# Flamingo block with routed experts: the last sums are taken into the experts' block

## What is computed

```python
x = x + tanh(g_xattn) * attention(layernorm(x), ctx)
t = layernorm(x)
top_w, top_i = top_k(softmax(t @ gate_w.T + gate_b), 2)
y = sum over the two choices of top_w * expert[top_i](t)
z = shared_expert(t)
x = x + tanh(g_ffn) * (y + z)
```

## Time and profile before

| | us |
|---|---|
| median of 3 runs | 618.12 |
| lowest, highest | 616.40, 619.42 |
| the profiled execution's own time | 621.78 |
| its span, first to last instruction | 619.8 |

### The profile page before, as it was taken

One profiled execution on the slowest core, in us unless ns is written; L12 is line 12 of the kernel. 1 busy time (PEld: TensorE's weight loads), 2 busy tenths in 40 slices (PEclk: granted clock), 3 DMA queues, 4 the chain that ended last, 5 costly groups with the idle time before them and its releaser, 6 DMA issues. The chain is left out here.

```text
span 619.8 us, 21883 instructions
## 1 busy us (share of the span) xinstructions
PE 491.7 (79%) x8747; PEld 415.3 (67%) x8747; DVE 417.3 (67%) x1246; ACT 324.5 (52%) x775; POOL 325.8 (53%) x454
## 2 busy tenths in 40 slices
PE   3889999899998998898776488999999999992000
PEld 2667777677777777776575377898889888982000
DVE  4677888688887888786933555676667666652166
ACT  2576877667776876775541224555555455552000
POOL 0012136466665675557777601776776776677000
PEclk9898999799999999998966599999999999997555
DMA  4222223334233243332112683466666665611398
GB/s 159 88 68 71 79 76 94 108 90 130 80 111 107 88 129 91 114 92 68 58 55 86 185 281 105 154 202 201 206 198 190 192 202 187 201 52 55 117 374 332
DMA packets 61221, 84.87 MB, mean 137 GB/s; under 512 B 11040, under 2 KB 36768, under 8 KB 60960
## 3 DMA queue, kind: packets, MB, share of 16 engines
q1 hardware_dynamic: 49552, 60.00, 31.3%
q0 software_dynamic: 8704, 17.97, 8.6%
q10 hardware_dynamic: 2864, 5.49, 2.5%
HBM read 52.89 MB, written 24.28 MB: 125 GB/s over the span
## 5 line engine op out<-in xcount | busy, mean ns | idle before, releaser
L1008 POOL DMA_INDIRECT expert_results<-YW,XB x144 | 138.1, 959 | 82.8 <-ACT YW L719 48.2
L957 POOL DMA_INDIRECT routed_rows<-STAGE,IDX x128 | 126.9, 991 | 41.6 <-issue 32.5
L719 ACT ACTIVATE YW<-YB,XB 128x128 f32<-128x128 f32 x144 | 46.0, 390 | 58.8 <-DVE YB L942 53.2
L628 ACT ACTIVATE PT<-BANKS 128x512 f32<-128x512 f32 x128 | 71.0, 614 | 8.6 <-PE BANKS L427 7.9
L427 PE MATMUL BANKS<-CST,LATE 128*128 128x128 f32 x512 | 73.9, 291 | 0.3 <-ACT PT L628 0.3
L427 PEld LDWEIGHTS BANKS<-CST,LATE 128*128 128x128 f32 x512 | 62.3, 150 | 10.9 <-issue 8.0
L970 POOL TENSOR_TENSOR VE<-MV,EPSV 128x4 f32<-128x4 f32 (+1 forms) x35 | 6.9, 196 | 116.9 <-DVE MV L755 116.8
L437 PE MATMUL BANKS<-VX,PT 128*32 128x18 f32 x4096 | 54.0, 188 | 10.5 <-issue 10.1
L760 DVE TENSOR_REDUCE MX<-BANKS 128x16 f32<-128x1024 f32 x32 | 39.1, 1222 | 30.0 <-PE BANKS L412 29.9
L628 ACT ACTIVATE VX<-BANKS 64x128 f32<-64x128 f32 x128 | 35.2, 275 | 45.6 <-PE BANKS L546 43.3
L437 PEld LDWEIGHTS BANKS<-VX,PT 128*32 128x32 f32 x4096 | 45.3, 112 | 19.4 <-issue 17.4
(11 more groups left out here) (113 smaller groups left out, 1032.8 us busy)
## 6 DMA issues: line engine op xcount, KB each, us to landing
LATE<-in_experts SPq DMA_DIRECT2D x72, 257.0 KB, 3.0
XB<-routed_rows SPq DMA_DIRECT2D x72, 130.0 KB, 3.0
XCT<-in_inputs_t SPq DMA_DIRECT2D x32, 256.0 KB, 2.9
YC<-expert_results SPq DMA_DIRECT2D x32, 256.0 KB, 5.8
X<-in_x SPq DMA_DIRECT2D x32, 128.0 KB, 3.1
LATE<-QK SPq DMA_DIRECT2D x128, 32.0 KB
out<-X ACTq DMA_DIRECT2D x16, 256.0 KB, 5.5
STAGE<-STAGE SPq DMA_DIRECT2D x6, 512.0 KB
```

The costliest lines, as they stand in the source:

```text
L628: return nc.scalar.activation(dst, src, ACT.Copy)
L719: nc.scalar.activation(YW[:, (j - 1) % 2, p, a, :], YB[:, p, a, :], ACT.Copy, scale=XB[:, (j - 1) % SLOTS, p, a, DIM:DIM + 1]).then_inc(yw ...
L957: nc.gpsimd.indirect_dma_start(routed[:, :], bass.IndirectOffsetOnAxis(ap=IDX[:, s, g.slots.start + t:g.slots.start + t + 1], axis=0), STA ...
L1008: nc.gpsimd.indirect_dma_start(results[:, :], bass.IndirectOffsetOnAxis(ap=XB[:, b, p, a, DIM + 1:DIM + 2].bitcast(i32), axis=0), YW[:, b ...
```

## The change

The second block is gone. Its three loops stand behind the experts' steps in the streams of SP, ACT and DVE of the first block, so that DRAIN and barrier between the two are gone as well.

- SP and ACT each wait for the eight sent semaphores (wait_results); POOL no longer does.
- YC and YSUM are views of the memory of STAGE, now one flat tensor STAGED of 6240 values on each partition, of which the views take 6144.
- The loads of the second choice (s = 1) of the first four steps are issued by ACT, and all others by SP as before.
- DVE's wait for out_ready of its own earlier step is dropped.
- The loops are written out over constants, with the same sixteen steps, sizes and four buffers.

```diff
-            STAGE = sa("STAGE", [128, TOPK, RING * UT, ROW])
+            STAGED = sa("STAGED", [128, TOPK * RING * UT * ROW])
+            STAGE = STAGED[:, :].rearrange("p (s r c) -> p s r c", s=TOPK, c=ROW)
+            wide = CBUFS * CG * DIM
+            YC = STAGED[:, 0:TOPK * wide].rearrange("p (b s a d) -> p b s a d", b=CBUFS, s=TOPK, d=DIM)
+            YSUM = STAGED[:, TOPK * wide:(TOPK + 1) * wide].rearrange("p (b a d) -> p b a d", b=CBUFS, d=DIM)
...
+            def load_results(engine, n, s):
+                engine.dma_start(YC[:, n % CBUFS, s, :, :], y_tiles[s, :, n * CG:(n + 1) * CG, :]).then_inc(y_in[n % CBUFS], 16)
+
+            def wait_results(engine):
+                for b in range(SLOTS):
+                    engine.wait_ge(sent[b], 64 * ((STEPS - b + SLOTS - 1) // SLOTS))
...
                 run_b(sp, expert_step)
+
+                wait_results(sp)
+                for n in range(CSTEPS):
+                    if n >= CBUFS:
+                        sp.wait_ge(ysum_done, n - CBUFS + 1)
+                    load_results(sp, n, 0)
+                    if n >= CBUFS:
+                        load_results(sp, n, 1)
...
                 run_b(act, expert_step)
 
+                wait_results(act)
+                for n in range(CBUFS):
+                    load_results(act, n, 1)
+                for n in range(CSTEPS):
+                    act.wait_ge(out_ready, n + 1)
+                    act.dma_start(out[:, n * CG:(n + 1) * CG, :], X[:, n * CG:(n + 1) * CG, :]).then_inc(stored, 16)
+                act.wait_ge(stored, 16 * CSTEPS)
...
                 run_b(dve, expert_step)
+
+                for n in range(CSTEPS):
+                    b = n % CBUFS
+                    dve.wait_ge(y_in[b], 32 * (n // CBUFS + 1))
+                    nc.vector.tensor_tensor(YSUM[:, b, :, :], YC[:, b, 0, :, :], YC[:, b, 1, :, :], ALU.add).then_inc(ysum_done, 1)
+                    here = X[:, n * CG:(n + 1) * CG, :]
+                    dve.wait_ge(ysum_done, n + 1)
+                    nc.vector.tensor_tensor(here, here, YSUM[:, b, :, :], ALU.add).then_inc(out_ready, 1)
...
                 run_b(pool, expert_step)
-                for b in range(SLOTS):
-                    pool.wait_ge(sent[b], 64 * ((STEPS - b + SLOTS - 1) // SLOTS))
```

More of the change, by code:

```diff
@@ L40 @@
 CG = 4
+CBUFS = 4
+CSTEPS = TILES // CG
 class Group:
@@ L246, in build_program @@
                  "yb_done", "yw_done", "sh_ready", "sgs_done", "hs_done", "z_ready", "zb_done", "x_done"))
+            y_in = [sem(f"y_in{b}") for b in range(CBUFS)]
+            ysum_done, out_ready, stored = sem("ysum_done"), sem("out_ready"), sem("stored")
+            y_tiles = results[0:TOPK * TOKENS, :].rearrange("(s p a) d -> s p a d", s=TOPK, p=128)
             block = own.enter_context(nc.Block())
+            def load_results(engine, n, s):
[3 more added lines that the diff above has]
+                    engine.wait_ge(sent[b], 64 * ((STEPS - b + SLOTS - 1) // SLOTS))
             def run(step):
```

## The result

The changed kernel takes 611.16 us (median of 8 runs, 607.25 to 613.63); the kernel before, with as many runs, takes 616.83 (614.69 to 620.42). The ratio is 0.9897, 95% interval 0.9863 to 0.9931: 4.3 to 8.5 us less. The profiled execution has a span of 609.0 us, against 619.8.

A forecast was written before the change was run, and what follows sets the result against it. It took an idle gap during POOL's DRAIN, slow first loads, then full DMA engines at 405 GB/s as the bounds. Gains 5.1 + 1.1 = 6.2 us, from median 618.12 to 611.9 us; range 608.5 to 615.5.

The forecast's parts named there:

- The hole: Between POOL's last scatter and the first load of YC: removing DRAIN and barrier gains 5.1 us, bounds 4.9 to 5.3.
- The hole stays: Before the first loads: the 4.65 us are not the DRAIN's own and remain; gain 1.6, 616.5 us, chance 0.09.
- DRAIN of some 4.6 us beside the loads: Sign expected in the profile after: POOL's DRAIN runs while the first loads move, not ahead of them.
- First loads on two queues: Start of the last sums: SP and ACT each issue four of eight first loads; gain 1.1 us, between 0 and 2.0.
- Taken: 290 GB/s: Rate assumed for the eight first loads: 2.95 MB at 10.3 us after first issue, 0.46 MB more, gain 1.1 us.
- both bounds: Limits for issuing the first loads from SP and ACT: gain 0 at 265 GB/s, 2.0 us at 395 GB/s.
- the upper bound: First loads at the kernel start's 395 GB/s: 3.30 MB at 10.3 us, 0.81 MB more, gain 2.0 us.
- barrier only: Last sums: reading limited at 265 GB/s, so faster issue only lengthens a queue; gain 5.1, 613.0 us, chance 0.24.
- Two queues are faster: First loads of the last sums: SP and ACT together reach the kernel start's 395 GB/s; gain 7.1, 611.0 us, chance 0.13.
- The slower case: Full DMA stretch: longer streams wait for their own instructions, three 7.9 us waits on SP; 623.6 us, chance 0.04.
- The waits on ACT: ACT waits for the sent semaphores before its four loads, its last product done ten us earlier; cost 0.
- the dropped wait of DVE: In the last sums, DVE's wait for its own sum of four steps earlier is removed; effect 0.

## Why the prediction was right, and where not

**The hole.** This part was right, in size and in cause. Foretold: 5.1 us, with 4.9 to 5.3 as bounds. Measured: 7.53 - 2.40 = 5.13 in the traces, and the same 7.53 or 7.54 in all four traces with two blocks, 2.40 to 2.42 in all traces where nothing waits for the DRAIN. That POOL's DRAIN is what fills it was an argument in the prediction and is shown now by putting it back: 4.8 of the 5.1 us return. "The hole stays" is out: the loads' data flow from 573.7 us on, 0.9 us after the first issue, while POOL's DRAIN lasts until 576.0. The sign "DRAIN of some 4.6 us beside the loads" came as one of 10.99 us, since it is recorded from before the last scatters.

**First loads on two queues.** This is the term that failed: 1.1 us foretold, and about 0.1 in the traces. From first load to end the three with one queue and no long issue take 36.3, 36.4 and 36.4 us, the four with four of the first loads on ACT and the same sums 36.0, 36.2, 36.4 and 36.5. By the medians 1.1 us is neither shown nor excluded. The step that went wrong is the one it was measured against: "Taken: 290 GB/s" and both bounds compare with 2.49 MB in the first ten us, and the 290 is itself the rate of that execution, the one with an issue of 1.79 us. Two others of the same kernel moved 3.03 and 3.04 MB, more than the 2.95 that two queues were to reach. What the prediction called in dispute, the rate with all eight loads issued, is 320 to 332 GB/s with one queue and 391 to 406 with two, near the 395 of the upper bound. A second queue does move more at first (3.17 to 3.25 MB against 2.91 to 3.04), 0.3 to 0.8 us at the full rate, but nothing of that can be seen at the last sum. Much of the lead is still there 32 us after the first issue, when 0.65 and 0.71 MB are left in the changed kernel and 0.78 and 0.82 in the later profiles of the kernel before; it goes in the last four us, where the DMA engines are no longer full (154 to 187 GB/s on the mean). The upper bound, 3.30 MB, wasn't reached in the changed kernel.

**The rivals.** What the runs show is most like "barrier only" in size, though not for its reason: 265 GB/s was no limit on reading, as one queue had 320 to 332 and two had 391 to 406. "Two queues are faster" holds for some ten us and not for the time. The rule of the Trainium skill, page "DMA: Bandwidth & Descriptors", section "Issuing engines are not separate DMA queues", that issuing from several engines saves only issue time, would have given no more than the term taken. The stretch to the end agrees with it (36.4 us with one queue, 36.2 and 36.5 with two); the rate after all eight issues, 332 and 393 GB/s, does not. The rule against which the 4.65 us were set, the Trainium skill's page "VectorE: DVE Perf Modes", section "The DRAIN you can't avoid", drains of about 12 ns around a kernel on all engines, is near ACT's last one (8 ns) and not near POOL's (4651 and 4648 ns), nor SP's and DVE's last ones (122 and 730 ns). The slower case did not show: in the full stretch no issue took over 0.91 us.

**The sum.** Foretold 611.9 us and a gain of 6.2; measured 611.16 and 5.7 between the medians. That the time is so near is in part luck, because two things cancel: the term of 1.1 us isn't there, and with 8 runs the kernel before has a median of 616.83, 1.3 us below that of its first three. 616.83 - 5.1 = 611.7 leaves 0.5 us, well inside the interval. The waits on ACT, the dropped wait of DVE and the shared memory were put at nothing, and no trace shows a cost: the end is 3.9 us in both.

## What to carry to other kernels

Where two blocks meet, look at the drains of every engine and at what the next block really needs: here it needed eight semaphores, and waited 4.65 us for POOL's DRAIN, of which it needed nothing. Such a join is seen as a stretch without any busy engine and without a byte moved, and its length can be read off almost to the tenth of a microsecond (5.1 foretold, 5.13 in the traces), while the medians could tell the whole gain only as 4.3 to 8.5. A slow issue or a low rate that one execution shows once is not a term of the sum until a second profile has it too. Bytes moved sooner are not time won either: here two queues moved the first loads faster, and the 12.6 MB were through no sooner.

## What was not expected of the hardware

POOL's DRAIN after its scatters takes 4.65 us, in two blocks and alone (4651 and 4648 ns), though every scatter has landed before it begins, and a further one right behind it takes 34 or 39 ns. Recorded from before the last scatters on, as in the seven traces where POOL waits for nothing at its end, it ends 4.6 to 4.7 us after the last one has left POOL. In the kernel before it begins only when the scatters have landed and ends 6.3 us after that point (575.12 and 581.45), so POOL's own wait ahead of it cost some 1.7 us of the hole: an estimate from these two ends, no run took the wait out alone. Whether any POOL work brings this on or only indirect DMAs was not tried.

The same eight loads of 256 KB, all issued and with no store among them, moved at 320 to 332 GB/s from SP's queue alone (three traces) and at 391 to 406 from SP's and ACT's (six traces), in the fifth us after the first issue.

The issue of a plain DMA takes 320 to 450 ns as a rule, with a longest one of 0.5 to 0.9 us in nine of the twelve traces and of 1.79 us in one.
